# A token tower on one core: the last stage's projection weights and first block of y loaded during the last state-space step

## The reference

```
h = attention(emb[x]) + bias
y_f, y_b = gated scans of layernorm(h), forward and backward   (512 channels each)
h = h + y_f @ out_w_f + y_b @ out_w_b                          (the projection)
p = layernorm(h) @ U1 ; g = gelu(p @ V1 + b1) ; q = g @ U2
out = h + q @ V2 + b2
```

## Time and profile before

| | us |
|---|---|
| three runs | 3584.38, 3590.87, 3606.5 |
| their median | 3590.87 |
| the profiled execution | 3582.52 |
| its span | 3580.7 |
| last step's y store issued | 3329.65 |
| last stage's first DMA issued | 3334.85 |
| first projection matmul | 3354.73 |
| last instruction ends | about 3576.8 |

### The profile page before, as it was taken

The page is one execution under the profiler, slowest core; times in us unless marked ns, Lnnn a source line. Parts: engine busy times, 40 slices in busy tenths (PEclk is TensorE's granted clock), DMA queues, the critical chain, the costliest instruction groups (busy, mean ns, idle before and its releaser), DMA issues. The chain is left out here.

```text
span 3580.7 us, 69905 instructions
## 1 busy us (share of the span) xinstructions
PE 3289.7 (92%) x23969; PEld 1916.8 (54%) x23969; DVE 2889.6 (81%) x2818; ACT 2784.3 (78%) x4727; POOL 1569.5 (44%) x1443
## 2 busy tenths in 40 slices
PE   7699999999999999868999999999999999998698
PEld 4233333333333333344767677767677776776465
DVE  2699999899989999363889988888888988899222
ACT  2178888788878888815999998899889899999143
POOL 3100000000000000003999898899888988989100
PEclk9689999899989999989999999999999999999899
DMA  5430211202020200050111111111111111111431
GB/s 176 104 39 5 42 26 19 40 6 40 6 40 6 40 5 5 6 180 30 48 53 55 49 60 60 66 66 53 55 48 60 60 60 54 54 54 60 155 112 53
DMA packets 95178, 192.41 MB, mean 54 GB/s; under 512 B 17856, under 2 KB 32992, under 8 KB 93344
## 3 DMA queue, kind: packets, MB, share of 16 engines
q1 hardware_dynamic: 83376, 173.23, 17.6%
q10 hardware_dynamic: 9968, 10.89, 1.0%
q0 software_dynamic: 1536, 4.20, 0.6%
HBM read 136.63 MB, written 51.12 MB: 52 GB/s over the span
## 5 line engine op out<-in xcount | busy, mean ns | idle before, releaser
L1187 POOL TENSOR_TENSOR m_g<-m_hs,m_cb 128x512 f32<-128x512 f32 x1024 | 1300.7, 1290 | 170.7 <-DVE m_hs L1322 162.2
L575 DVE TENSOR_REDUCE a_mx<-a_ps_m 128x2 f32<-128x1024 f32 x1024 | 1242.1, 1224 | 83.0 <-PE a_ps_m L433 60.8
L551 ACT ACTIVATE a_probs<-a_ps_s 128x512 f32<-128x512 f32 x2048 | 1111.5, 596 | 196.2 <-PE a_ps_s L463 143.0
L1322 DVE TENSOR_TENSOR_SCAN m_hs<-m_da,m_carry,m_ps_x 128x512 f32<-128x512 f32 x768 | 952.7, 1268 | 119.7 <-PE m_ps_x L1211 83.1
L433 PE MATMUL a_ps_m<-a_k,a_q 48*128 48x512 f32 x2048 | 768.7, 468 | 34.6 <-DMA a_q<-q_scr 20.0
L463 PE MATMUL a_ps_s<-a_q,a_k 50*128 50x512 f32 x2048 | 771.5, 456 | 12.7 <-issue 6.0
L1211 PE MATMUL m_ps_x<-m_ident,m_bu 128*128 128x128 f32 x4096 | 636.7, 279 | 98.1 <-DVE m_hs L1322 87.0
L1267 ACT ACTIVATE m_bu<-m_dut,m_bt 128x512 f32<-128x512 f32 x896 | 639.8, 714 | 107.7 <-PE m_ps_x L1211 104.7
L1282 ACT ACTIVATE m_da<-m_delta,m_a_cur 128x512 f32<-128x512 f32 x1024 | 723.1, 712 | 0.2
L1211 PEld LDWEIGHTS m_ps_x<-m_ident,m_bu 128*128 128x128 f32 x4096 | 487.2, 143 | 430.6 <-issue 313.2
L470 PE MATMUL a_ps_o<-a_probs,a_v 128*32 128x256 f32 x8192 | 663.8, 396 | 8.7 <-ACT a_o L538 8.3
(11 more groups left out here) (138 smaller groups left out, 2316.6 us busy)
## 6 DMA issues: line engine op xcount, KB each, us to landing
m_cb<-c_scr SPq DMA_DIRECT2D x128, 512.0 KB, 3.7
y_scr<-m_ysb SPq DMA_DIRECT2D x16, 1024.0 KB, 6.7
ffn_y<-y_scr SPq DMA_DIRECT2D x16, 1024.0 KB, 7.4
a_k<-k_scr SPq DMA_DIRECT2D x96, 128.0 KB, 6.6
a_q<-q_scr SPq DMA_DIRECT2D x96, 128.0 KB, 8.5
q_scr<-p_partsq SPq DMA_DIRECT2D x16, 512.0 KB, 3.3
k_scr<-p_partsk SPq DMA_DIRECT2D x16, 512.0 KB, 3.3
m_xn<-xn_scr SPq DMA_DIRECT2D x16, 512.0 KB, 5.0
```

The costliest lines, as they stand in the source:

```text
L551: nc.scalar.activation(probs[:, t % PR, HEADS[j]], turned(i), ACT.Exp, scale=float(DK) ** -0.5).then_inc(exped, 1)
L575: nc.vector.reduce_max(mx[:, i:i + wide], ps_m[:, b:b + wide], AX.X).then_inc(m_maxed, 1)
L1187: nc.gpsimd.tensor_tensor(g[:, t % NG], hs[:, t % NHS], cb[:, quarter % 2, n % CQ], ALU.mult).then_inc(g_ok, 1)
L1322: nc.vector.tensor_tensor_scan(hs[:, t % NHS, rev], da[:, t % NDA, rev], ps_x[:, t % NX, rev], carry[:, n, i:i + 1] if p else 0.0, ALU.mul ...
```

## The change

`win`, `xn` and `xc` are allocated around both stages. The last stage's `wo` becomes a view of `win`, and chunk 0's y a view of `xn` (forward half) and `xc[:, 0]` (backward half). In the last step, behind the issue of C's quarter 6, SP issues four DMAs into them (two of `wo`, two of y; 3 MB) after three waits that make sure that the tiles are finished with and the y rows are stored. At the stage's end SP waits for them. The last stage loads neither: its SP begins with chunk 0's h alone (on a semaphore `h_in` of its own), then chunk 1, then chunk 2, whose y no longer waits; ACT begins with the nine small DMAs; PE waits for no transfer before chunk 0's projection.

```diff
+                def load_next():
+                    wo_next, y_next = handed_over(kept)
+                    sp.wait_ge(filled, number[STEPS - 1, Z + NTB - 1] + 1)
+                    for z in range(2):
+                        sp.dma_start(wo_next[:, z * ND:(z + 1) * ND], ow_t[z]).then_inc(next_in, 16)
+                    sp.wait_ge(stored, 16 * (STEPS - NC))
+                    sp.wait_ge(summed, (STEPS - 1) * TILES)
+                    for z in range(2):
+                        sp.dma_start(y_next[z], y_scr[z][0, :, 0:CH].rearrange("(k p) s -> p k s", p=P)).then_inc(next_in, 16)
...
                         if h == 6 and s + 1 < STEPS:
                             store_c(s + 1)
+                        if h == 6 and s == STEPS - 1:
+                            load_next()
...
                 sp.wait_ge(stored, 16 * STEPS)
+                sp.wait_ge(next_in, 16 * 4)
...
+def handed_over(kept):
+    win, xn, xc = kept
+    return (win.rearrange("p k (n d) -> p (k n) d", d=D), [xn.rearrange("p a k s -> p (a k) s"), xc[:, 0]])
...
-                    if n >= 2:
+                    if n > 2:
                         sp.wait_ge(h_ps[1], 2 + n - 1)
...
-                for n in range(3):
+                sp.dma_start(h[:, 0], h_scr[0:4].rearrange("t p d -> p t d")).then_inc(h_in, 16)
+                for n in range(1, 3):
                     load(n)
...
-                        pe.wait_ge(y_in[buf], ONE + (n - buf) * 24 + 48)
+                        if not first:
+                            pe.wait_ge(y_in[buf], ONE + (n - buf) * 24 + 48 * buf)
                         pe.wait_ge(h_ok[half], ONE + n)
...
-                pe.wait_ge(wo_in, ONE + 2 * 16)
                 for t in range(4):
-                    project(0, 0, t)
+                    project(0, 0, t, True)
...
-                for z in range(2):
-                    act.dma_start(wo[:, z * ND:(z + 1) * ND], ow_t[z]).then_inc(wo_in, 16)
                 act.dma_start(bias2[:, :], b2.partition_broadcast(P)).then_inc(w_in, 16)
...
                     dve.wait_ge(h_ps[0], ONE + n + 1)
-                    dve.wait_ge(y_in[buf], ONE + (n - buf) * 24 + 48)
+                    if first:
+                        dve.wait_ge(h_in, ONE + 16)
+                    else:
+                        dve.wait_ge(y_in[buf], ONE + (n - buf) * 24 + 48 * buf)
```

More of the change, by code:

```diff
@@ L624, with attention_out_and_mamba @@
 CAP = 20.0
-def attention_out_and_mamba(nc, sem, o_scr, wo, bo, h_scr, dirs, win_t, xp_t, dtw_t, xn_scr, y_scr, c_scr):
+def attention_out_and_mamba(nc, sem, o_scr, wo, bo, h_scr, dirs, win_t, xp_t, dtw_t, xn_scr, y_scr, c_scr, kept, ow_t):
     with ExitStack() as ctx, ExitStack() as ctx_out, ExitStack() as ctx_steps:
@@ L650, in attention_out_and_mamba @@
         ident = sb("ident", [P, P], FP32)
-        win = sb("win", [P, KD, 2 * DI], FP32)
+        win, xn, xc = kept
         wxp = sb("wxp", [P, 2, ND, XPW], FP32)
@@ L657, in attention_out_and_mamba @@
         taps = sb("taps", [P, 2, ND, DC - 1, P], FP32)
-        xn = sb("xn", [P, 2, KD, CH], FP32)
         xh = sb("xh", [P, ND, HB + CH + HB], FP32)
@@ L661, in attention_out_and_mamba @@
         nothing = sb("nothing", [P, ND, HB], FP32)
-        xc = sb("xc", [P, 2, ND, CH], FP32)
         zs = sb("zs", [P, 2, NTB, DI], FP32)
@@ L699, in attention_out_and_mamba @@
         g_ok, summed, y_ok = s_("g_ok"), s_("summed"), s_("y_ok")
-        stored = s_("stored")
+        stored, next_in = s_("stored"), s_("next_in")
         ow_in, eps_ok = sem("o_w_in"), sem("o_eps_ok")
@@ L1332, in _, with mamba_out_and_ffn @@
                     gate(STEPS - 1, i)
-def mamba_out_and_ffn(nc, sem, y_scr, ow_t, h_scr, u1, v1, b1, u2, v2, b2, out):
+def handed_over(kept):
+    win, xn, xc = kept
+    return (win.rearrange("p k (n d) -> p (k n) d", d=D), [xn.rearrange("p a k s -> p (a k) s"), xc[:, 0]])
+def mamba_out_and_ffn(nc, sem, y_scr, kept, h_scr, u1, v1, b1, u2, v2, b2, out):
     NF = FF // P
@@ L1347, in mamba_out_and_ffn @@
         ident = sb("ident", [P, P], FP32)
-        wo = sb("wo", [P, NY, D], FP32)
+        wo, y_first = handed_over(kept)
         wu1 = sb("u1", [P, KD, 2 * RK], FP32)
@@ L1376, in mamba_out_and_ffn @@
         w_in, cleared, ident_ok, eps_ok = s_("w_in"), s_("cleared"), s_("ident_ok"), s_("eps_ok")
-        wo_in = s_("wo_in")
-        y_in = [s_("y_in0"), s_("y_in1")]
+        h_in, y_in = s_("h_in"), [s_("y_in0"), s_("y_in1")]
         h_ps = [s_("h_ps0"), s_("h_ps1", 2)]
@@ L1429, in _, with project @@
             def _(pe):
-                def project(n, buf, t):
+                def project(n, buf, t, first=False):
                     half = t // 2
                     if t % 2 == 0:
-                        pe.wait_ge(y_in[buf], ONE + (n - buf) * 24 + 48)
+                        if not first:
+                            pe.wait_ge(y_in[buf], ONE + (n - buf) * 24 + 48 * buf)
                         pe.wait_ge(h_ok[half], ONE + n)
                     for k in range(NY):
-                        last = nc.tensor.matmul(ps_h[:, t], y[:, buf, k, t * P:(t + 1) * P], wo[:, k],
-                                                start=k == 0, stop=k == NY - 1)
+                        turned = y_first[k // ND][:, k % ND, t * P:(t + 1) * P] if first else y[:, buf, k, t * P:(t + 1) * P]
+                        last = nc.tensor.matmul(ps_h[:, t], turned, wo[:, k], start=k == 0, stop=k == NY - 1)
                     if t % 2:
@@ L1554, in _, with first_half @@
             def _(dve):
-                def first_half(n, buf):
+                def first_half(n, buf, first=False):
                     dve.wait_ge(h_ps[0], ONE + n + 1)
-                    dve.wait_ge(y_in[buf], ONE + (n - buf) * 24 + 48)
+                    if first:
+                        dve.wait_ge(h_in, ONE + 16)
+                    else:
+                        dve.wait_ge(y_in[buf], ONE + (n - buf) * 24 + 48 * buf)
                     nc.vector.tensor_tensor(h[:, buf, 0:2], ps_h[:, 0:2], h[:, buf, 0:2], ALU.add).then_inc(h_ok[0], 1)
@@ L1599, in _ @@
                 dve.wait_ge(w_in, ONE + 9 * 16)
-                first_half(0, 0)
+                first_half(0, 0, True)
                 second_half(0, 0)
@@ L1626, in lm_tower @@
             attention(nc, sem, q_scr, k_scr, v_all, o_scr)
[L1627 to L1633, removed]
+    with nc.sbuf_tensor("m_win", [P, KD, 2 * DI], FP32) as win, nc.sbuf_tensor("m_xn", [P, 2, KD, CH], FP32) as xn, \
+            nc.sbuf_tensor("m_xc", [P, 2, ND, CH], FP32) as xc:
+        kept = (win, xn, xc)
+        with semaphores(nc) as sem:
+            attention_out_and_mamba(nc, sem, o_scr, a["L0_tok_wo"], a["L0_tok_bo"], h_scr,
+                                    dirs, win_t, xp_t, dtw_t, xn_scr, y_scr, c_scr, kept, ow_t)
+        with semaphores(nc) as sem:
+            mamba_out_and_ffn(nc, sem, y_scr, kept, h_scr, a["L0_ffn_U1"], a["L0_ffn_V1"], a["L0_ffn_b1"],
+                              a["L0_ffn_U2"], a["L0_ffn_V2"], a["L0_ffn_b2"],
+                              out.rearrange("b (t p) d -> (b t) p d", p=P))
 def laid_out(name, value):
```

## The result

Sixteen executions of the changed kernel have a median of 3570.39 us (3560.93 to 3589.55), those of the kernel before 3590.07 us (3574.14 to 3606.5). The ratio is 0.9946, with a 95% interval of 0.9930 to 0.9963: 13 to 25 us of 3590, where 17 were forecast; the time forecast was 3574. The profiled execution took 3565.47 us against 3582.52, 17.05 less.

The account below looks back on a forecast made before the run. Bound: at the stage boundary PE waited for chunk 0's y and h, then worked through the chunks, with `w_in` late next. Gain 17.1 less 0.1 to 0.4, about 17 us: median 3590.87 to 3574, range 3564 to 3588.

Parts of the forecast that it names:

- PE's start: Last stage: chunk 0's projection waits only for semaphore start values and begins at 3335.5, 19.2 us earlier.
- Chunk 0's projection: PE's 64 records after its start: 13.8 us plus 2.45 for the low clock, 16.3 us, to 3351.8.
- `w_in`: Nine small weight DMAs land at 3353, the middle between 3348.2 and 3357.2 (all packets paired from 3337).
- Transposes: Chunk 0's transposes on PE start at 3360.8 instead of 3377.9, 17.1 us earlier.
- Chunk 1's y and h: Chunk 1's loads on SP's queue, put at 3353, the same time as `w_in`.
- Sum: Whole kernel: 17.1 us less 0.1 to 0.4 for added work, about 17 us gained.
- lower bound: `w_in` at 3348.2: 1664 packets alone 2.4 us, V1 1.9 us, then 1152 paired packets 7.9 us.
- The clock in the new wait: PE's clock stays up in its 2 us wait before chunk 1; rival, it falls: gain 14.7 us, chance 0.30.
- What follows: Chunk 2's h in by 3368.5, its projection not before 3371.8: nothing comes back, 3 us to spare.
- the added work: Last step: four early DMAs cost POOL at most 0.3 us, semaphore and wait 0.1; quarter 7 lands 7 us early.
- `w_in` at 3361.9: Rival: weights land as late as before, PE idles 10 us, gain 5.9 us; 0.15, shared with unseen losses.
- PE without a wait: Rival: `w_in` by 3348.2 and chunk 1's y by 3351.8, gain 19.2 us, 3572; chance 0.13.

Follow-up runs that it names:

- e11: The changed kernel itself, profiled and timed again: 3579.15 us, ratio 0.9966 to the kernel before; last stage 224.10 us.
- e10: The change, but `wo` loaded in the last stage again, at the head of SP's queue: last stage 233.58 us.
- e8: The kernel before, plus one wait so ACT issues the nine weight DMAs after chunk 0's y and h land: last stage 234.63 us against 241.90.
- e7: The change, plus one wait so SP issues chunk 1's and chunk 2's loads only when all weights are in: last stage 230.24 us.
- e3: The change with its four early DMAs issued three times, each round after the last landed: last stage 224.40 us, C's last quarter 13.29 us late.
- e5: The change with chunk 2's y waiting for chunk 0's projection again: last stage 225.02 us.
- e4: The change with the waits for `w_in` moved behind chunk 0's normalization, first copy and transposes: last stage 227.47 us.
- e1: The change with only chunk 0's y loaded early; `wo` back at the head of ACT's queue in the last stage: last stage 235.12 us.
- e6: The change, plus a wait so ACT issues the nine weight DMAs only after chunk 0's h lands: last stage 234.13 us.
- e9: The change with chunk 1's y loaded early too, behind C's quarter 5, and chunk 2's y waiting again: 3573.43 us, ratio 0.9948; last stage 222.08 us.

## Why the prediction was right

*PE's start*: 3335.5 forecast, 3335.85 measured. *Chunk 0's projection*: 16.3 us forecast, 15.5 measured (3335.85 to 3351.4); the low clock lasted to 3338.9, about 3 us at half speed instead of some 4.5, so the 2.45 us reckoned for it were about 1.6. *`w_in`*: 3353 forecast, 3352.89 measured (3340.49 + 12.40); the stage began 0.42 us later here, so counted from S it was 0.5 us early. *Transposes*: 3360.8 forecast, 3360.90 measured in the chain. *Chunk 1's y and h*: 3353 forecast, 3353.2 measured. *Sum*: 17 us forecast, 17.05 measured between the profiled executions. The medians differ by 19.7 us, those beside e11 by 12.0; both intervals hold the 17, so it is the trace and not the time that confirms it to the us. The prediction held that a measurement of this kernel tells about 1%; with sixteen runs of each the interval is 0.33% wide, and no change (a ratio of 1) lies outside it.

The agreement on `w_in` is better than the steps behind it, and luck in part. I took the middle between a lower bound with a long lead and an upper one with none. The trace goes by the steps of the lower bound (3348.2), and they were 4.7 us short together, 0.4 of it the later start. The first 1664 packets (b2, U1, b1) were out at about 3339, not at 3338.4: the short runs were faster alone than the 697 per us of the earlier trace rows (896 packets in the 0.6 us from 3338.0), but only 80 packets went out before 3337. The lead was not the silence of over 3 us that I had read from the earlier trace rows: h0 was issued at 3337.39, and SP's queue had its first packets 1.1 us later. The page of the Trainium skill that I set against the row there, "DMA: Bandwidth & Descriptors", section "Latency and other measured facts", gives some 600 ns to the first byte. The 1.1 us measured here is nearer to that than to my reading. The step that failed most is V1: 0.5 MB in some 5 us (3340 to 3345), where I had reckoned 1.9 from the rate of the earlier trace rows; and the one packet each of the earlier trace rows does not hold there (611 to 185). The last 1152 packets took the 7.9 us that were forecast (3345 to 3352.9). That the middle lay 4.8 us above the lower bound had another reason, some pairing during the lead. e10, e8 and e7 show that the order at the head of the queues and the sharing behind it set these landings; what made V1 slow they do not show.

*The clock in the new wait* was forecast to stay up, and did in the profiled execution. That was not as safe as I had it. PE's waits before chunk 1 and what the clock did: 0.71 us (e11), 1.61 (e3), 2.36 (the change) and 2.79 (e5), full clock kept; 2.18 (e4), 3.66 (e7), 5.38 (e1) and 8.47 (e6), fallen. Between 2 and 3 us it went both ways, so the 0.30 given to a fall was not idle, and the length of the wait alone doesn't decide.

*What follows* and *the added work*: nothing came back later (26.60 us a chunk), and POOL paid 0.03 us a product during the burst. The rivals: `w_in` at 3361.9 did not happen because q10 had its lead; e1 is what it looks like when the lead is lost. PE without a wait is e9.

Where I was wrong is in the experiments: in e1 I had `w_in` hidden behind PE's records with `wo` ahead of it, in e10 and e7 I let the order change for nothing, as if the load that was put back would not come later itself.

## What to carry to other kernels

When a stage starts by loading, look for two landings, the first operand and the last of the small constants, and ask which is late once the other is cured. Here small transfers shared the DMA engines with large ones, one packet each for much of the time, so what stood at the head of a queue in the first few microseconds decided more than its bytes: with the same bytes `w_in` came 8.9 us earlier (e10 against e1), and one wait that orders the loads (e8) gave 7 us of 17 with no prefetch. Tiles that a stage finishes early were free buffers for the next, as long as what queues behind the early loads (here C's last quarter) has slack of its own (7 us in the change).

## What was not expected of the hardware

Runs of 4 bytes and 256 bytes went at 1011 packets in one us with 17 of the other queue beside them. V1, 128 rows of 4 KB into 64 partitions at a time, was far slower: in the change 0.5 MB took some 5 us, with SP's queue moving more packets than ACT's; in the stretches of e7 and e9 in which it ran it went at about 0.1 MB per us also. Why was not tried. And the granted clock fell after a wait of 2.18 us but not after one of 2.79.
